# A two-layer graph attention kernel: where in a step TensorE makes the first projection group

## The reference

```python
def layer0(x, adj):                                  # 128 graphs, 64 nodes, 384 features
    q, k, v = x @ Wq + bq, x @ Wk + bk, x @ Wv + bv   # split into 12 heads of 32
    scores = q @ k.T / sqrt(32) + beta * adj
    scores = where(adj > 0, scores, -9e15)
    return softmax(scores) @ v
def layer1(x, adj):
    q, k, v = x @ Wq.T, x @ Wk.T, x @ Wv.T + bv
    a = q @ k.T * 384 ** -0.5 + adj                  # rows that are zero throughout give 0
    return (softmax(a) @ v) @ Wo.T + bo
x = layernorm(x + layer0(x, adj))
x = layernorm(x + layer1(x, adj))
```

## Time and profile before

| | |
|---|---|
| three runs, median | 1075.25 us |
| the profiled execution | 1069.95 us |
| its span | 1068.2 us |
| granted clock of TensorE, mean | 0.994 of full speed |
| TensorE busy | 1036.6 us, 97% |
| VectorE busy | 795.1 us, 74% |
| GpSimd busy | 784.5 us, 73% |
| ScalarE busy | 449.1 us, 42% |
| chain that ended last | TensorE 89%, VectorE 4%, GpSimd 3% |

### The profile page before, as it was taken

How to read it: one execution, slowest core, us unless ns; L and a number is a source line. 1 busy time by engine, 2 the same in 40 slices (tenths; PEclk the granted TensorE clock), 3 DMA queues, 4 the chain that set the end, 5 groups by cost and what they waited for, 6 DMA issues and landing times.

```text
span 1068.2 us, 38489 instructions
## 1 busy us (share of the span) xinstructions
PE 1036.6 (97%) x16896; PEld 898.2 (84%) x16896; DVE 795.1 (74%) x1582; ACT 449.1 (42%) x713; POOL 784.5 (73%) x642
## 2 busy tenths in 40 slices
PE   6999999999999999999999999999999999999975
PEld 5887888888888888888888888888888888888864
DVE  3587777868778686886868778687786868777784
ACT  4554434444343444443444344443444444344421
POOL 1588777777787786777778777786877778777675
PEclk9999999999999999999999999999999999999997
DMA  6421112112111121112112111121111210010100
GB/s 207 139 71 52 35 42 67 39 44 62 44 39 47 36 62 44 40 46 58 48 44 62 37 46 40 44 62 44 40 46 40 66 44 2 26 27 10 35 32 31
DMA packets 61750, 53.33 MB, mean 50 GB/s; under 512 B 35984, under 2 KB 55440, under 8 KB 61584
## 3 DMA queue, kind: packets, MB, share of 16 engines
q1 hardware_dynamic: 60752, 49.69, 15.7%
q10 hardware_dynamic: 832, 1.18, 0.3%
HBM read 38.28 MB, written 12.58 MB: 48 GB/s over the span
## 4 chain that ended last, share of the span: by engine, by line
PE 89%; DVE 4%; POOL 3%; issue 2%; DMA 1%; ACT 1%; POOLq 0%; DVEq 0%
PE ps_u L361 54%; PE ps_h L361 9%; PE ps_s L379 8%; PE ps_s L449 8%; PE ps_h L468 7%; PE ps_h L397 2%; PE ps_h L480 2%; POOL probs L781 1%; DMA xt_in<-in_x_t 1%; DVE row_sum L691 1%; ACT probs L572 1%; DVE probs L650 1%; DVE row_max L659 1%; POOL probs L787 0%; POOL xt_lo L807 0%
## 5 line engine op out<-in xcount | busy, mean ns | idle before, releaser
L781 POOL TENSOR_TENSOR probs<-probs,row_max 128x768 f32<-128x768 f32 x128 | 193.2, 1509 | 226.8 <-DVE row_max L659 226.8
L787 POOL TENSOR_TENSOR probs<-probs,row_inv 128x768 f32<-128x768 f32 x128 | 193.3, 1510 | 2.5 <-DVE row_inv L695 2.5
L691 DVE TENSOR_REDUCE row_sum<-probs 128x12 f32<-128x768 f32 x128 | 122.0, 953 | 65.8 <-ACT probs L572 65.8
L541 ACT COPY probs_t<-ps_s 128x768 f32<-128x768 f32 x128 | 102.7, 802 | 111.1 <-PE ps_s L449 111.0
L361 PE MATMUL ps_u<-w_hi_v,xt_lo 128*128 128x384 f32 x384 | 137.8, 359 | 0.0
L361 PE MATMUL ps_u<-w_hi_v,xt_hi 128*128 128x384 f32 x384 | 129.4, 337 | 0.0
L361 PE MATMUL ps_u<-w_lo_v,xt_hi 128*128 128x384 f32 x384 | 129.1, 336 | 0.0
L659 DVE TENSOR_REDUCE row_max<-probs 128x12 f32<-128x768 f32 x128 | 121.3, 948 | 2.2
L361 PE MATMUL ps_u<-xt_hi,w_lo_q 128*128 128x512 f32 x285 | 121.6, 427 | 0.0
L572 ACT ACTIVATE probs<-probs 128x768 f32<-128x768 f32 x128 | 108.5, 848 | 29.0 <-POOL probs L781 27.1
L361 PE MATMUL ps_u<-xt_hi,w_lo_k 128*128 128x512 f32 x288 | 118.2, 410 | 0.7 <-ACT q_sb L560 0.7
(11 more groups left out here) (78 smaller groups left out, 2090.6 us busy)
## 6 DMA issues: line engine op xcount, KB each, us to landing
x_in<-in_x SPq DMA_DIRECT2D x16, 768.0 KB, 4.5
out<-z SPq DMA_DIRECT2D x64, 192.0 KB, 2.0
xt_in<-in_x_t SPq DMA_DIRECT2D x15, 768.0 KB, 4.6
adj<-in_adj SPq DMA_DIRECT2D x64, 128.0 KB, 3.1
xt_in<-in_x_t SPq DMA_DIRECT2D x3, 256.0 KB, 4.7
q_sb<-in_wq ACTq DMA_DIRECT2D x3, 192.0 KB, 4.9
k_sb<-in_wk ACTq DMA_DIRECT2D x1, 576.0 KB, 7.5
v_sb<-in_wv SPq DMA_DIRECT2D x1, 576.0 KB, 7.0
```

The source lines that it names most:

```text
L541: nc.scalar.copy(probs_t[:].rearrange("p (a i) n -> p a (i n)", a=2), ps_s[:, 0:2, 0:KT * P]).then_inc(probs_t_ready, 1)
L691: nc.vector.reduce_sum(row_sum[p][:], probs[p][:].rearrange("p i b k -> p (i b) k"), AX_X)\
L781: nc.gpsimd.tensor_tensor(s, s, over_keys(row_max[p]), ALU.subtract).then_inc(shifted, 1)
L787: nc.gpsimd.tensor_tensor(s, s, over_keys(row_inv[p]), ALU.mult).then_inc(probs_ready, 1)
```

## The change

In TensorE's loop over the steps, the loop that makes the first unit moves from behind the scores to behind the turned probabilities. All units of a step then stand in a row there. The loops of the other engines are as before, and so are all waits.

```diff
--- before.py
+++ after.py
@@ -490,14 +490,14 @@
             for s in STEPS:
                 if s.cur:
                     scores(s.cur)
-                for unit in s.units[:1]:
-                    make_unit(unit)
                 if s.last:
                     result(s.last)
                 if s.turned:
                     turn_activations(s.turned, s.last)
                 if s.prev:
                     turn_probs(s.prev, s.cur)
+                for unit in s.units[:1]:
+                    make_unit(unit)
                 for unit in s.units[1:]:
                     make_unit(unit)
                 if s.prev:
```

## The result

The changed kernel takes 1287.01 us (median of 4 runs, 1276.65 to 1289.22) against 1073.91 us before (4 runs, 1071.02 to 1076.05): 1.198 times as long, with a 95% interval of 1.194 to 1.201. That is 213 us more. The forecast was 1243 us, 170 us more. The direction was right and so were the three waits, but the size fell short by a fifth. The measured time lies 1 us inside the overall range of 1165 to 1288 and outside the 1220 to 1265 that the forecast gave itself; it is nearer to rival B, the fallen clock, at 1275.

What follows compares the result with a forecast made beforehand. TensorE's own work, busy 97%, was taken as the bound; waits add 11.2 us per pair of phases (75.6 against 64.37), 179 for 16 pairs, taken as 170, giving 1243 us. Own range 1220 to 1265, overall 1165 to 1288.

Steps and rivals of the forecast that it cites:

- rival B: TensorE's clock also falls for 4 us ahead of turned probabilities at layer 1 t=0, costing 32 more: 1275; 12%.
- heads wait: Layer 1: result waits for the heads' low part (line 708) on VectorE, starting at best 1.31 us after scores start.
- bias wait: Turned probabilities wait for VectorE's 1.01 us bias addition, starting 1.91 us after scores start, without the unit's cover.
- queue wait: ScalarE's copy of the late first unit holds back casts, turned probabilities' copy, exponential; 8.80 us period in layer 0.
- The v copy ahead of the residual: Steps t=3: VectorE copies the late first v unit before residual and sums; 8.4 us in layer 0, 9.3 in layer 1.
- the eight steps: One layer-0 phase and one layer-1 phase, four steps each: 75.6 us forecast against 64.37 before, 11.2 more per pair.
- Rival A: Queue wait delays nobody; only bias wait and heads wait count: the eight steps take 69.5 us, the whole 1155; 10%.
- Rival C: At `turn_probs`, turned probabilities are ready one unit earlier and all behind moves up: 1044 to 1075; 3%.
- the room that the weight loads' share seemed to leave: Skill's rule on TensorE: 84% weight-load share leaves 16% of the span, 171 us, where waits could vanish: no change.
- Rival D: Waits of one step are paid back by a long step behind: +6 to +9 per pair, 1170 to 1220; 15%.
- my t=3 reckoning: At t=3 of layer 0, GpSimd's scaling path gives 8.4 us between turned probabilities; VectorE's next bias ends at 8.2.

Runs made afterwards that it cites:

- copies behind, mask later: Changed kernel with ScalarE's and VectorE's first-unit copies moved later in their queues, and the layer-0 mask moved behind the next step's row maxima: 1170.30 us.
- the filled kernels: Extra unread TensorE matmuls in waits: changed kernel with 9, 5, 3: 1259.66 us; with 7 and 3 more: 1249.31; VectorE's first-v copy later, filled: 1230.94.
- ScalarE's copy alone: Changed kernel with only ScalarE's copy of a step's first unit moved behind the exponential: 1231.04 us.
- both copies behind: Changed kernel with the first unit's copy moved behind the exponential on ScalarE and behind the sums on VectorE: 1203.79 us.

## Why the prediction was right, and where it fell short

The 213 us, by differences of medians; in the first row 1071 is the kernel before as timed beside it, so that the rows add up to 216:

| part | us | from |
|---|---|---|
| heads wait, and the late v copy at t=3 of layer 1 | 51 | unit between result and turned probabilities: 1122 - 1071 |
| bias wait, less the late v copy | 48 | copies behind, mask later: 1170 - 1122 |
| mask ahead of the bias, with its clock | 34 | 1204 - 1170 |
| queue waits of the two copies, with their clock | 83 | 1287 - 1204 |

The rows are not pure. From the first kernel to the second, TensorE's order, the copies and the mask all differ: the bias wait comes in, and at t=3 of layer 1 the 0.7 us of the late v copy go. At t=0 of layer 1 the scaling and not the bias sets 10.2 us. The parts would also differ in another order of taking them out: VectorE's copy is worth 4 us alone, 18 with the clock filled and 27 once ScalarE's copy has moved.

*Three waits, point by point.* The bias wait: forecast as P = T+1.91; in the kernel with the mask later, the steps that it alone sets (t=2 and t=3 of layer 0, t=1 of layer 1) are 8.62, 6.55 and 7.51 us long, where the forecast's lengths give 8.6, 6.5 and 7.5. The heads wait of layer 1, a result at T+1.31: in its own experiment the result starts 1.32 us after the scores, with 0.54 us of wait, right. The queue wait, a period of 8.80 in layer 0: measured 8.81 and 8.84; with ScalarE's copy moved, t=1 takes 7.51 and t=2 8.65, which is TensorE's own length. The v copy ahead of the residual is shown for t=3 of layer 1, which shrank by 1.3 us when it moved. For t=3 of layer 0, 8.4 against 8.60, it is only argued: with the copy moved the period was 8.86, as the bias behind the mask ended last there instead. The forecast had these two limits 0.2 us apart, without the longer mask.

*The term that was mis-sized* is the clock, which the sum put at nothing. The forecast reckoned the eight steps at full clock, 75.6 us, and kept the fallen clock as rival B with 12%, at one place per pair and 2 us. In fact it fell at two places per pair, at t=0 of layer 1 and between t=3 of layer 1 and t=0 of layer 0. The measured 2.9 us per pair are the surplus in the table above, and the filled kernels show that the time comes back when the clock does. The forecast had named a granted clock under 0.97 as a sign that it was wrong, and 0.953 is that. The second place had been in my own lengths, with a wait for the low part of the activations and one for the low part of the heads close together; I looked at the largest wait only. That the time still lies in the overall range, by 1 us, is owed to rival B's share in it and to luck.

*The ends.* The alternating part has 13 pairs of phases, not 16; the other six phases are the ends. The forecast's 170 us are thus 146 for the 13 pairs at 11.2 and 24 for the ends. The 104 steps in the middle went from 838.5 to 1020.6 us, 182 us or 14.0 per pair, and the steps ahead of them and behind them, from the first scores to the last, from 180 to 214 us, so 34 us. So 36 us of the shortfall lie in the regular part and 10 in the ends. The clock takes a part of the ends too: t=0 of the second and third phase took 13.1 and 14.5 us.

*Rival A* (only TensorE's own waits, 1155) is what the kernel with copies behind and mask later came near to, 1170. For the change as it stands it was wrong: ScalarE's low busy share, 42% before, said nothing of the order in its queue. It also left out the mask at t=0 of layer 1, though the forecast had it in its own sum. *Rival C* (not slower) and the room that the weight loads' share seemed to leave did not come true: that share fell from 84% to 73%, and the time rose all the same. *Rival D* (slack repays a part): two of the eight steps came out under their forecast, by 0.1 us, so next to nothing was repaid.

*What was named for the profile after.* TensorE's busy share near 84%: 85%, but from a busy time 56 us longer than it reckoned, in a span some 45 us longer. Waits of the turned probabilities on L787 at t=1, 2 and 3 of layer 0: none at t=1, where the late result of layer 1 comes last, and 1.97 and 0.92 at t=2 and t=3. At t=0 of layer 1 I had named the bias; it is the scaling that ends last, with 2.43 us, as my t=3 reckoning had the two within 0.2 us of each other. Waits of the result on L708, about 0.6 us and more: 0.54 at the shortest (t=1 of layer 0), 0.72, 1.03 and 1.20 at the others. Scores at t=1 and t=2 of layer 0 some 8.8 us apart: they are 8.5 and 10.0 apart; it is the turned probabilities that have the period of 8.8.

## What to carry to other kernels

When the order of one in-order engine is changed, go through the queues of the engines that consume its work: an instruction that used to be ready when its turn came can hold back all that stands behind it in its queue, and it then couples steps that had been independent. Work that stands between a producer's two dependent groups is worth as much as the waits that it covers, even on an engine that is 97% busy. When a reordering opens waits on TensorE, price its clock too, at every place where waits come close together, and in a further experiment give it harmless work in the waits, no longer than they are, to see what the clock costs.

## What the hardware showed that was not expected

The mask's second operation on VectorE reads two tensors of SBUF. It took 0.75 us in the kernel before and 1.83 us in the kernels with the copies behind, for the same 128x512 elements. In the first case it started within `normalise` (L819) on GpSimd and ahead of the scaling; in the second it started within the scaling, a tensor-tensor operation. Here are VectorE and GpSimd of the kernel before, then GpSimd of the kernel with both copies behind, beside the mask at 503.12 shown above:

```profile
441.61 0.75 DVE L620 SCALAR_TENSOR_TENSOR bias<-adj,beta_col,bias 128x512 f32<-128x512 f32 x1
```

```profile
440.30 1.66 POOL L819 TENSOR_SCALAR x<-z,mean_var,rstd 128x384 f32<-128x384 f32 x1
441.93 1.77 POOL L787 TENSOR_TENSOR probs<-probs,row_inv 128x768 f32<-128x768 f32 x1
```

```profile
502.78 1.63 POOL L783 TENSOR_TENSOR probs<-probs,row_inv 128x768 f32<-128x768 f32 x1
```

The mask ends at 504.95, 0.54 us behind the scaling's end at 504.41. In the kernel before it was the scaling that was longer, 1.77 in place of 1.48 us, starting at 441.93 within the mask. The mask's second operation takes the same every time from 200 to 900 us of the traces: 0.75 us in the kernel before, the changed one and the one with ScalarE's copy alone, 1.83 to 1.85 in those with VectorE's copy behind. The Trainium skill, SBUF — State Buffer, SBUF: two separate sides, says that VectorE operations with two SBUF inputs and GpSimd operations that read SBUF take a shared pair of ports as an exclusive lock, the loser waiting for the whole instruction. The trace agrees for the scaling, in both orders. It does not for `normalise`: that had started 1.31 us ahead and ended within the mask, and the mask still took 0.75 us, so not every GpSimd operation locks it out. GpSimd's spans are rough, and no experiment here isolated the cause.

The other surprise is how readily lost clock moves: with three waits filled, it fell at a fourth (0.85 over t=2 of layer 0), and an improvement of VectorE's queue worth some 18 us at a clock near full was worth 4 us, no more than the runs scatter, with the clock free to fall.
